# Four groups of images in another split: 6, 6, 10, 10 in place of 6, 10, 10, 6

## What is computed

```python
h = tok(x)                          # patches @ W.T, class token ahead: 32 x 37 x 192
h = concat([cls_tok, h])
y = norm(h)
# attention block, on y
k, v = ln1(y) @ Wk.T, ln1(y) @ Wv.T; sr = sigmoid(ln1(y) @ Wr.T)
y = y + (sr * bi_wkv(decay / T, first / T, k, v)) @ Wo.T     # two scans over the 37 tokens
y = y + sigmoid(ln2(y) @ Wr_f.T) * (square(relu(ln2(y) @ Wk_f.T)) @ Wv_f.T)
h = h + y
# experts, on norm(h): 4 groups of 4, best 2 groups, best 4 experts of them
h = h + sum_e c[t, e] * expert_e(norm(h)) + shared(norm(h))
```

## Time and profile before

| | us |
|---|---|
| median of 3 runs | 259.08 (258.5 to 260.05) |
| the profiled execution | 259.53 |
| its span, first to last instruction | 257.6 |
| PE busy with matmuls | 245.2 |
| DVE busy | 191.2 |
| ACT busy | 151.5 |
| POOL busy | 17.1 |

### The profile page before, as it was taken

The page is one execution under the profiler, slowest core; times in us unless marked ns, Lnnn a source line. Parts: engine busy times, 40 slices in busy tenths (PEclk is TensorE's granted clock), DMA queues, the critical chain, the costliest instruction groups (busy, mean ns, idle before and its releaser), DMA issues.

```text
span 257.6 us, 4492 instructions
## 1 busy us (share of the span) xinstructions
PE 245.2 (95%) x1508; PEld 222.6 (86%) x1508; DVE 191.2 (74%) x491; ACT 151.5 (59%) x312; POOL 17.1 (7%) x26
## 2 busy tenths in 40 slices
PE   6988879999999998999999999999999999999994
PEld 4866458578588898999999999999999999999993
DVE  4459988999989998999797799887333175853542
ACT  2399798988868998853795971426441432132220
POOL 5100202003101000101100000101000010000000
PEclk9999999999999999999999999999999999999998
DMA  5668563000000342000003520000144000015500
GB/s 154 211 191 286 212 186 119 0 3 0 0 0 6 84 111 57 0 3 0 1 3 121 187 76 4 1 3 0 54 163 158 29 3 0 1 23 109 102 29 26
DMA packets 13015, 17.49 MB, mean 68 GB/s; under 512 B 2336, under 2 KB 11074, under 8 KB 12866
## 3 DMA queue, kind: packets, MB, share of 16 engines
q1 hardware_dynamic: 12722, 17.11, 22.3%
q10 hardware_dynamic: 272, 0.11, 0.2%
HBM read 16.22 MB, written 0.99 MB: 67 GB/s over the span
## 4 chain that ended last, share of the span: by engine, by line
PE 74%; DVE 9%; ACT 9%; issue 3%; DMA 2%; POOL 0%; SPq 0%; DVEq 0%; POOLq 0%; ACTq 0%
PE PG L964 18%; PE PA L984 17%; PE PG L966 11%; PE PF L984 7%; PE PQ L964 4%; PE PQ L966 3%; PE PX L1001 2%; PE PF L1001 2%; ACT norm L417 2%; DMA w_tok<-in_w_tok 2%; PE PF L974 1%; PE PG L1119 1%; PE PG L1118 1%; DVE K L763 1%; PE PF L991 1%
## 5 line engine op out<-in xcount | busy, mean ns | idle before, releaser
L575 ACT ACTIVATE act<-PG,columns 128x222 f32<-128x222 f32 (+3 forms) x56 | 28.4, 507 | 59.0 <-PE PG L966 45.9
L964 PE MATMUL PG<-stack,hi_egu 128*128 128x222 f32 (+1 forms) x288 | 62.2, 324 | 0.0
L913 DVE SCALAR_TENSOR_TENSOR hid<-PG,columns,act 128x222 f32<-128x222 f32 (+1 forms) x52 | 27.3, 524 | 29.3 <-PE PG L966 26.7
L984 PE MATMUL PA<-w_ed,hid 128*124 128x192 f32 (+1 forms) x240 | 46.1, 327 | 0.6 <-DVE hid L922 0.5
L964 PEld LDWEIGHTS PG<-stack,hi_egu 128*128 128x128 f32 x288 | 45.7, 191 | 0.9 <-DVE hid L913 0.4
L966 PE MATMUL PG<-stack,lo_egu 128*128 128x222 f32 (+1 forms) x192 | 42.8, 304 | 0.0
L984 PEld LDWEIGHTS PA<-w_ed,hid 128*124 128x124 f32 (+1 forms) x240 | 38.6, 183 | 1.3 <-issue 1.3
L966 PEld LDWEIGHTS PG<-stack,lo_egu 128*128 128x128 f32 x192 | 31.8, 191 | 0.0
L391 POOL TENSOR_TENSOR rstd<-var,minus_half 112x2 f32<-112x2 f32 (+3 forms) x12 | 13.8, 1146 | 191.7 <-DVE var L657 191.7
L922 DVE TENSOR_TENSOR hid<-hid,gates 128x222 f32<-128x222 f32 (+1 forms) x48 | 21.9, 461 | 1.6 <-DMA gates<-c_rows 0.7
L984 PE MATMUL PF<-w_down,mix_hid 128*124 128x192 f32 (+1 forms) x120 | 22.8, 326 | 0.0
(11 more groups left out here) (248 smaller groups left out, 441.3 us busy)
## 6 DMA issues: line engine op xcount, KB each, us to landing
gates<-in_w_egu SPq DMA_DIRECT2D x6, 512.0 KB, 4.9
gates<-c_rows SPq DMA_DIRECT2D x16, 138.8 KB, 2.9
gates<-c_rows SPq DMA_DIRECT2D x16, 92.5 KB, 2.7
gates<-c_rows SPq DMA_DIRECT2D x16, 83.2 KB, 2.5
w_ed<-in_w_ed SPq DMA_DIRECT2D x1, 1152.0 KB, 6.1
gates<-c_rows SPq DMA_DIRECT2D x16, 55.5 KB, 2.5
gates<-in_w_up SPq DMA_DIRECT2D x2, 384.0 KB, 4.5
pat<-in_patches SPq DMA_DIRECT2D x2, 370.0 KB, 4.3
```

Source lines behind the costliest of these rows:

```text
L575: nc.scalar.activation(act[128 - gate:128, n % 2, 0:G.n], PG[0:gate, gate_bank(n), 0:G.n], ACT.Silu, bias=bias).then_inc(act_silu, 1)
L913: V_.scalar_tensor_tensor(out, PG[part, 1, 0:G.n], bias, act[part, i, 0:G.n], ALU.add, ALU.mult).then_inc(mul_done, 1)
L964: mm(out, w_hi[:, slot, cols], x[:, p, 0:G.n], start=(p == 0), stop=False, skip_group_check=True)
L984: last = mm(tile_out(P, G, t), src[:, G.ts[t]:G.ts[t] + G.tp], w, start=start and t != 1, stop=stop, skip_group_check=True)
```

## The change

The groups get 6, 6, 10 and 10 images. All sizes that derive from `GROUP` follow: group 1 now has 222 tokens and two tiles, group 3 has 370 tokens, three tiles and two rounds. The maximum sizes of buffers stay. `Zt` keeps one buffer for each size. The three lists are written anew. The lists have the steps `F3:tok1`, `F3:o1`, `F3:x11` in place of `F1:tok1`, `F1:o1`, `F1:x11`; otherwise the same steps stand in another order. SP's order of DMAs, the tracks and POOL's order are the same.

```diff
-GROUP = [Group(0, 6), Group(6, 10), Group(16, 10), Group(26, 6)]
+GROUP = [Group(0, 6), Group(6, 6), Group(12, 10), Group(22, 10)]
...
-        Zt = {G.n: sb(f"Zt{G.n}", [128, G.n]) for G in GROUP[:2]}
+        Zt = {n: sb(f"Zt{n}", [128, n]) for n in dict.fromkeys(G.n for G in GROUP)}
...
-                    for s in (slice(0, min(G.wk, 512)), slice(512, G.wk))[:1 + g]:
+                    for s in (slice(0, 512), slice(512, G.wk)) if G.wk > 512 else (slice(0, G.wk),):
...
 PE_ORDER = _order(
-    "H:early0 H:early1 H:early2 H:early3 F0:tok0 H:early4 H:early5 H:tok H:stats0 H:stats1 H:aggr H:var H:rstd F0:tr1a",
-    "F0:tr1b F1:tok0 F1:tok1 F0:k F0:kt F0:v F0:rt F0:r H:scan0 H:scan1 H:sb0 H:sb1 H:e1 H:edge F0:sub0 F0:sub1 F0:sub2",
...
-    "D1:d5 G1:v7 G1:g8 D1:d6 G1:v8 G1:g9 M2:tr3 F3:o0 G1:v9 M2:logits D1:d7 D1:d8 G1:g10 G1:v10 D1:d9 G1:g11 D1:d10 G1:v11",
-    "G1:g12 M3:tr2 G1:v12 G1:g13 D1:d11 D1:d12 G1:v13 D2:cT M3:rf M3:up0 D1:d13 M3:up1 M3:mix0 G2:g0 G2:g1 M3:up2 M3:mix1",
...
+    "H:early0 H:early1 H:early2 H:early3 F0:tok0 H:early4 H:early5 H:tok H:stats0 H:stats1 H:aggr F0:tr1a F0:tr1b F1:tok0",
+    "F0:k F0:kt F0:v F0:rt F0:r H:var H:rstd H:scan0 H:scan1 H:sb0 H:sb1 H:e1 H:edge F0:sub0 F0:sub1 F1:tr1a F0:sub2",
...
+    "G1:g8 G1:v8 G1:g9 F3:o0 G1:v9 G1:g10 D1:d7 F3:o1 D1:d8 G1:v10 M2:tr3 G1:g11 G1:v11 D1:d9 M2:logits G1:g12 G1:v12",
+    "D1:d10 D1:d11 G1:g13 G1:v13 M3:tr2 D1:d12 G2:g0 G2:g1 D1:d13 M3:rf G2:v1 D2:cT G2:g2 G2:v2 M3:up0 G2:g3 G2:v3 D2:d1",
...
 DVE_ORDER = _order(
...
-    "F3:sum F3:sum2 F3:den S1:s5 F3:recip0 X1:x5 M2:gated S1:s6 M2:h1 X1:x6 M2:stats3 M2:aggr3 M2:var3 S1:s7 X1:x7 M2:ln3",
-    "F3:recip1 F3:z S1:s8 M2:tr3a X1:x8 M2:tr3b F3:x10 F3:x1 M2:high M3:stats2 M2:logits M2:score S1:s9 M2:scores X1:x9",
...
+    "F3:sum X1:x5 F3:sum2 S1:s6 F3:den X1:x6 F3:recip0 F3:recip1 M2:gated S1:s7 F3:z M2:h1 S1:s8 M2:stats3 X1:x7 M2:aggr3",
+    "M2:var3 F3:x10 X1:x8 M2:ln3 S1:s9 X1:x9 F3:x11 F3:x1 S1:s10 M2:tr3a M2:tr3b M3:stats2 M3:aggr2 S1:s11 M2:high M3:var2",
...
```

## The result

The changed kernel takes 266.51 us (median of 4 runs, 265.7 to 266.97) against 259.12 of the kernel before on the same chip: ratio 1.0279, 95% interval 1.0238 to 1.0319. The forecast was 263.0 us, with a range from 260.5 to 265.3: the sign was right, the size 3.5 us short. The profiled execution took 266.7 us with a span of 264.9. In what follows a median is over all executions of a kernel, and a ratio leaves out single ones that took over 1.5% longer than the fastest of the same kernel.

A forecast was written before the change was run, and what follows sets the result against it. DVE's list was taken to bind up to about 124 us, PE's from there. M2's router at 161.35 plus 99.5 us of PE, third point agreeing, taken as 261.0; tail 0.5, span 261.5; plus 1.5 gives 263.0 us, range 260.5 to 265.3.

The forecast's parts named there:

- three points: M1's router, M2's router, and M2's routing with D2:cT: each falls at the later of DVE's and PE's lists.
- M1's router: First meeting point: DVE's list brings it from 124.6 to 111.3 us.
- DVE's content ahead: DVE's work before M1's router: falls by 13.3 us, of which 9.9 from F1.
- "at nothing": F3's second round through PX (tok1, o1, x11): no cost, bounded by a wait of 0.5 us a round.
- M2's router: Second meeting point: DVE's list reaches it at 161.3 us, PE's own content near 155, so PE stands idle.
- the term of closed idle time: DVE idles 6.0 us from 124 to 166 us; 3.8 of it closes ahead of M2's router.
- the one on content: DVE's work ahead of M2's router: 1.6 us less in all.
- M2's router to the last addition: Behind M2's router PE has the old 90.8 us and 8.7 more.
- The tail: After the last product: 0.3 us for the last S and X steps plus the addition's second bank; 0.5 us added.
- A: PE's content alone decides, M1's router being the last binding point: faster, 256.3 us; chance 0.09.
- B: Lists mesh better: all 6.0 us of DVE idle time close, 0.5 us kept at start: 260.2 us; chance 0.15.
- C: PE's clock falls at the start without the last two spins: 264 to 266 us; chance 0.09 above 265.3.

The follow-up runs named there:

- b_norecip1: The kernel before without the two reciprocals of group 1 (3.7 us of DVE ahead of M1's router): 258.75 us, ratio 0.9982.
- a_patches: store_112 with group 3's patches loaded ahead of group 0's 24 gate transfers in SP's order: 262.58 us, ratio 1.0126; again 262.84, 1.0151.
- b_patches: The kernel before with group 3's patches moved ahead of group 0's gate transfers in SP's order: 258.31 us, ratio 0.9943.
- spins_norecip13: spins_back without the four reciprocals of groups 1 and 3 (6.0 us of DVE ahead of M2's router): 264.19 us.
- spins_back: store_112 with the two spins H:var and H:rstd again ahead of F0:tr1a, as in the kernel before: 264.52 us, ratio 1.0224.
- store_112: The changed kernel with each tile of the last group stored by two DMAs, first 112 rows and the rest: 264.75 us, ratio 1.0206.
- a_m0_both: store_112 without group 1's two reciprocals and the 12 low-part products of M0's up steps: 262.35 us, ratio 1.0103.
- p_ab3_m2: a_patches without group 3's two reciprocals and two backward scans and the 12 low-part products of M2's up steps: 261.89 us, ratio 1.0105.
- store_106_old: The kernel before with its last group's two tiles stored as 106 + 6 and 106 + 4 rows: 262.72 us, ratio 1.0134.
- p_m1_both: a_patches without group 2's two reciprocals and the 12 low-part products of M1's up steps: 260.98 us, ratio 1.0063.
- new_split_old_lists: The kernel before with the new group sizes and store_112's store, its old order lists kept but for small edits: 282.52 us, ratio 1.0895.

## Why the prediction was right in sign and short in size

**What bounds the kernel: half right.** I had DVE's list as the bound up to 124 us and took the later list at three points. The engines were as full as I read them, but "DVE's list sets the pace" was wrong: b_norecip1 takes 3.7 us of it and gains 0.6 us with an interval that includes no change. The lists are tied by crossings every few microseconds (`gated` after `mix5`, S after G, `rf` after `tr2`), at which both arrive nearly together.

**M1's router: 2.5 us late.** Busy times up to the router, before and after:

```profile
0.00:124.62 124.62, 116.23 (x656) 95.37 (x657) 108.87 (x245) 96.37 (x194) 13.72 (x22) 1.00 0.27 84
```

```profile
0.00:113.84 113.84, 101.80 (x590) 83.11 (x591) 97.22 (x233) 89.60 (x188) 13.15 (x22) 1.00 0.30 92
```

DVE's content ahead fell by 11.65 us, not 13.3: the term was 1.65 too large; in which of its parts isn't shown. Its idle time rose from 15.75 to 16.62, by 0.9. The move in SP's queue gives back 1.0 to 1.1 us in the changed kernel (a_patches), but 0.7 in the kernel before as well (b_patches), so of the rise the queue explains 0.3 to 0.4; the rest has no run. The prediction put group 3's second round "at nothing" with 0.5 us a round as its bound, and said that SP's order stays as it is. It does; but the patches are now 370 KB in place of 222, land 3.5 us behind their issue in place of 3.0, and meet a fuller DVE list.

**M2's router: 1.8 us early, and its closeness proves little.** By 159.58 us DVE has done 97.22 + 44.51 = 141.73 us:

```profile
113.84:159.58 45.74, 44.70 (x316) 42.66 (x315) 44.51 (x109) 31.30 (x64) 1.70 (x2) 1.00 0.15 35
159.58:257.30 97.72, 96.67 (x593) 94.27 (x591) 47.38 (x150) 30.48 (x60) 2.18 (x2) 1.00 0.17 53
```

Before, it was 108.87 + 36.15 (of 42.20) = 145.02. So 3.3 us less content (I had 1.6) and 166.82 - 145.02 = 21.80 us of idle time against 17.85, 3.95 closed (I had 3.8). 166.82 - 3.3 - 3.95 = 159.6. So the term of closed idle time came out in the sum (4.8 us closed between the routers, 0.9 opened ahead of them), and the one on content was 1.7 too small. But the mechanism behind both, that DVE's list sets this point and PE waits for it, isn't borne out: 6.0 us less of DVE's list left the point where it was (spins_norecip13, 160.21, and 160.3 in spins_back). PE's content ahead of it fell by 11.9 us (146.50 for 158.43, forecast 11.6), so that part was right, and PE's holes grew by 4.7; 3.65 of these lie ahead of M1's router already, and in the 45.74 us between the routers PE has only 1.04. That the forecast came near is luck in part: content and waits of two tied lists were put into one of them.

**M2's router to the last addition: +0.9.** PE's content there grew from 86.78 to 96.67 us, 9.9 where I had 8.7. PE from M1's router on has 141.38 us of work against 128.98, 12.4 where I had 10.0. Which price was too low isn't shown: a five-pass product costs 0.85 us with 370 columns and 0.56 with 222 (134.97 to 135.82, 94.92 to 95.48 in the changed kernel), a `mix` step 0.84 and 0.52, and these are the differences that I had. DVE also waits 1.78 us for group 3's gates at 228.51 us (0.75 before).

**The tail: the step that failed.** The prediction added 0.5 us for the last S and X steps and the second bank, and took the store with the old 3.3 us. Its last DMAs stood in no term, though they are in the chain that ends the kernel and the change alters their row counts from 112 and 110 to 124, 122 and 124. It cost 4.3 us: 4.03 from the first issue on (6.76 for 2.73), 0.26 in the addition. store_112 gives back 2.9 of the 4.03 by the row counts alone. With this term the forecast would have been 261.5 + 4.3 = 265.8 of span, 267.3 us, 0.8 us above the result; that too rests on the errors ahead of it, which cancel.

**The rivals.** A (PE's content alone, faster) would have needed M2's router before 157.6 us; only a_m0_both and p_ab3_m2, with about 3.6 and 8.0 us of work left out (by the costs above), came there (both at 157.49). B (better mesh) had the closed idle time at 6.0 us; it was 3.95, and the store would have hidden it anyway. C (clock) happens, in other executions. Its number, 264 to 266 us, was nearest to the result, by a mechanism that wasn't at work in it.

## What to carry to other kernels

Follow the chain to its very last instruction, and when a change alters the shape of what is stored last, price the transfer by its row count, not by its bytes: tiles of 124, 122 and 124 rows ended the kernel 4 us later than two of 112 and 110 did. When an engine looks like the bound, look for the crossings inside its stage before pricing work on it at its full time; two lists that are both about 95% full can be tied, as here, and work taken from one becomes a wait for the other. Price left-out products by the distance of their starts, not by the length of their records. A queue whose order doesn't change still has to be priced if the consumer moves forward.

## What the runs showed of the hardware

- Stores of 106, or of 122 and 124, rows of 768 bytes keep the DMA engines at one to two tenths, and the span ends 6.0 and 6.8 us behind the first issue (store_106_old, the changed kernel); with 110 or 112 rows the share is up to eight tenths and the end comes after 2.7 and 3.9 us (the kernel before, store_112).
- The granted clock fell from 1.00 to 0.50 (1.2 GHz) for some 6.5 us at the end of a hole of PE of 1.74 us (store_112; 1.56 us in p_m1_both) at 16 to 18 us, and was back at 1.00 by 25 us. In new_split_old_lists it fell between 158 and 159 us, in a hole of 1.33 us that came 1.4 us behind one of 2.61, and was back by 166. Holes of 1.55 us (at `F0:tr1a`) and of 1.44 us (at `M1:rf`) in the changed kernel left it at 1.00.
- Two products in a row take 0.34 us with 370 columns and 0.22 us with 222, from the first one's start to that of the next step, though the record of each one lasts 0.33 and 0.28 us.
- The start is uneven from one execution to the next: the first scan starts at 19.3 us in the profile of before, at 18.0 in b_norecip1 and at 17.8 in the changed kernel, while its engines wait for loads; so a point of one profile is known to about 1 us, and distances between two points (45.74, 45.74, 45.75) much better.
